# Writing out the batch loops of the attention heads on every engine of a one-core attention and expert kernel

## What is computed

```python
# B, S = 8, 512;  H = 256;  NH = 16;  NOPE, ROPE, VD = 128, 64, 128;  QR, KVR = 128, 64
norm_q  = rmsnorm(x @ W_cq, q_scale)
q_nope, q_rope = norm_q @ W_dq_nope, norm_q @ W_dq_rope        # per head
norm_kv = rmsnorm(x @ W_ckv, kv_scale)
k_nope, value = norm_kv @ W_dk_nope, norm_kv @ W_dv            # per head
k_rope  = x @ W_krope                                          # one for all heads
query = concat([q_nope, rope(q_rope)]);  key = concat([k_nope, rope(k_rope) / NH])
scores = where(causal, query @ key.T / sqrt(NOPE + ROPE), -1e9)
out = softmax(scores) @ value @ W_o                            # 16 heads, 8 batches
x = x + out + ffn(layernorm(x))                                # experts and shared expert
```

## Time and profile before

| what | value |
|---|---|
| median of three runs | 1854.5 us (1851.81 to 1855.62) |
| profiled execution, its own time | 1855.27 us |
| span of the profiled execution | 1853.5 us |
| mean granted clock of PE | 0.895 |
| busy: PE, PEld, DVE, ACT, POOL | 1467.5, 1248.0, 1115.1, 930.9, 569.7 us |

### The profile page before, as it was taken

How to read it: one execution, slowest core, us unless ns; L and a number is a source line. 1 busy time by engine, 2 the same in 40 slices (tenths; PEclk the granted TensorE clock), 3 DMA queues, 4 the chain that set the end, 5 groups by cost and what they waited for, 6 DMA issues and landing times. The chain is left out here.

```text
span 1853.5 us, 37109 instructions
## 1 busy us (share of the span) xinstructions
PE 1467.5 (79%) x10112; PEld 1248.0 (67%) x10113; DVE 1115.1 (60%) x4335; ACT 930.9 (50%) x2739; POOL 569.7 (31%) x640
## 2 busy tenths in 40 slices
PE   2663499989899999999999986799998888885340
PEld 2552378868688777878878764588887777774330
DVE  2896276656566676766666644555555666664464
ACT  1330276656566666666666644366665555552000
POOL 1120043433343343433433430000001433335565
PEclk8676699999999999999999997799999998998665
DMA  3993611321411111111111107654545665665553
GB/s 143 329 375 123 232 56 56 113 88 47 147 58 60 49 52 60 58 62 58 58 54 47 50 21 239 201 163 157 159 153 163 197 184 183 193 194 179 148 168 112
DMA packets 169539, 240.29 MB, mean 130 GB/s; under 512 B 16786, under 2 KB 142738, under 8 KB 165010
## 3 DMA queue, kind: packets, MB, share of 16 engines
q1 hardware_dynamic: 146322, 183.61, 29.9%
q0 software_dynamic: 18432, 50.36, 8.8%
q10 hardware_dynamic: 4608, 4.20, 0.8%
HBM read 115.42 MB, written 122.68 MB: 128 GB/s over the span
## 5 line engine op out<-in xcount | busy, mean ns | idle before, releaser
L988 ACT ACTIVATE prob<-prob,negmax 128x512 f32<-128x512 f32 (+3 forms) x512 | 285.3, 559 | 302.1 <-DVE negmax L1066 300.8
L1066 DVE CUSTOM_DVE_ANT_0 prob<-ps,mask_add 128x512 f32<-128x512 f32 (+3 forms) x512 | 244.2, 485 | 147.4 <-issue 144.2
L61 PE MATMUL ps<-kt_hi,qt_hi 128*128 (+4 forms) x512 | 188.5, 368 | 21.7 <-issue 18.7
L816 POOL DMA_INDIRECT sorted_x<-xn_row,row_no x192 | 188.3, 981 | 49.4 <-issue 45.0
L826 POOL TENSOR_TENSOR spread<-rinv,one 128x512 f32<-128x512 f32 x64 | 66.6, 1040 | 380.0 <-DVE rinv L1072 380.0
L63 PE MATMUL ps<-kt_hi,qt_lo 128*128 (+4 forms) x512 | 166.4, 325 | 0.0
L62 PE MATMUL ps<-kt_lo,qt_hi 128*128 (+4 forms) x512 | 166.0, 324 | 0.0
L910 PE MATMUL ps<-ident,prob 128*128 128x128 f32 x1280 | 160.6, 273 | 0.0
L926 PE MATMUL ps<-pt,nkv 128*64 128x512 f32 (+3 forms) x1024 | 152.0, 439 | 2.3 <-DVE lat L1084 2.3
L910 PEld LDWEIGHTS ps<-ident,prob 128*128 128x128 f32 x1280 | 143.5, 140 | 0.2 <-ACT prob L988 0.2
L1001 ACT ACTIVATE pt<-ps 128x1024 f32<-128x1024 f32 (+2 forms) x130 | 130.4, 1003 | 19.8 <-PE ps L910 16.9
(11 more groups left out here) (240 smaller groups left out, 4481.4 us busy)
## 6 DMA issues: line engine op xcount, KB each, us to landing
sorted_x<-zeros SPq DMA_DIRECT2D x16, 2048.0 KB, 9.4
rows_in<-sorted_x SPq DMA_DIRECT2D x128, 256.0 KB, 2.8
sorted_y<-rows_out SPq DMA_DIRECT2D x128, 256.0 KB
nqt<-nqt_dram SPq DMA_DIRECT2D x16, 512.0 KB
raw_gu<-in_wgu SPq DMA_DIRECT2D x16, 384.0 KB, 4.0
x_in<-in_x SPq DMA_DIRECT2D x8, 512.0 KB, 4.2
xn_dram<-xn SPq DMA_DIRECT2D x8, 512.0 KB, 5.0
xnt_dram<-xnt_hi SPq DMA_DIRECT2D x16, 256.0 KB, 4.7
```

The source lines that it names most:

```text
L61: pe.matmul(out, lh, rh, start=first, stop=False, **kw)
L816: pool.indirect_dma_start(sorted_x, bass.IndirectOffsetOnAxis(ap=row_no[par][:, k:k + 1], axis=0), xn_row[par][:], None).then_inc(scattere ...
L988: act.activation(prob[:, i, qt, 0:w], prob[:, i, qt, 0:w], ACT.Exp, bias=negmax[:, i, qt:qt + 1], scale=-1.0, accum_out=rowsum[:, g // 2 % ...
L1066: dve.tensor_tensor_reduce(prob[:, i, qt, 0:w], s_ps[k % 2][:, 0:w], mask[:, S - w:S], -1.0, -MASKED, ALU.add, ALU.min, negmax[:, i, qt:qt ...
```

## The change

```diff
         def run(eng):
             def batches(first, last):
-                with eng.Fori(first, last) as b:
+                for b in range(first, last):
                     for g in range(NH // 2, NH):
                         step(Batches(b, None, b + 1), g)
                     for g in range(NH // 2):
```

## The result

The changed kernel takes 1821.82 us (median of four runs, 1820.2 to 1824.25), the kernel before 1853.15 us beside it (1850.81 to 1855.62). The ratio is 0.9832, 95% interval [0.9813, 0.9851], a gain of 31.3 us. A second comparison on another chip, where both kernels run faster, gave 1755.58 against 1784.45 us, ratio 0.9843 [0.983, 0.9857], a gain of 28.9 us.

What follows compares the result with a forecast made beforehand. PE was taken to fill the heads stage, stalling at jumps back for instructions. Jumps gave 27.57 us, all other terms 0: 1855.27 - 27.57 = 1827.7 us, given as 1827.5, range 1821 to 1836 us.

Steps and rivals of the forecast that it cites:

- Jumps back: Heads loop: removing six taken jumps on PE, VectorE and ScalarE saves 27.57 us, each priced against the 106.93 us stretch.
- the two rules weighed there: Jump price: about 108 ns per compare-and-branch, 0.65 us for six, or a block fetch at far taken branches, which was favoured.
- the first two were dear: First two heads jumps, 8.76 us each: instructions queue behind SP's two 2 MB zero fills.
- the third jump: Third jump back in the heads: costs PE 1.49 us idle, with VectorE named as releaser; priced 1.80 us.
- Register and branch instructions: Heads loop: REGISTER_ALU and ISA rows, such as 97 and 24 on PE per pass, lie behind queued matmuls; worth 0.
- part 5: Code behind the heads at other addresses: expert loop L1549 has PE branches of 76 to 220 ns, no stall; 0.
- Sequential fetch: Heads: seven bodies read once instead of one read seven times; body already fetched anew each pass, so price 0.
- Rival C: Heads: written-out code cannot be fetched fast enough, about 42 packets at 2.33 us each; slower, 1925.6 us; chance 0.04.
- The row load under the fills: Step 8 row load comes earlier, inside the fills in two batches: up to 4.1 us late, absorbed by GpSimd's idle 4.20 us; 0.
- Rival B: Saving comes, but the row load exceeds GpSimd's slack (1836 us) or a loop behind the heads stalls (1838 us); chance 0.12.
- rival A: Heads turns: the jump costs only the branch, the stall is a wait for late data and stays; 1854.8 us; chance 0.03.
- Place of the code behind: Code behind the heads at other addresses: 0, upper end 3.56 us for each of three taken jumps of L1549 and L1552.

Runs made afterwards that it cites:

- padded: Changed kernel with GpSimd's batch loops kept and 352 one-element memsets per pass added to its body; 1760.21 us, against 1755.14 us for the control with GpSimd written out too.

## Why the prediction was right

**Jumps back, 27.57 us.** Right. The stretch that crosses the same turn without a jump was the right yardstick: its 106.93 us are the 106.95 us of every written-out pass. Measured: 27.42 us in the profiles compared. That the two agree to 0.2 us says no more than this, since both take the 776.1 us from the same profile of the kernel before. What the term did not say is that it is one execution's figure. The second profile of that kernel has 22.4 us over the same yardstick; about 3 us of the difference lie at jumps that held PE in one of the two and not in the other.

**The time itself** came out 5.7 us below the forecast, with a mechanism that is right. 1.9 us of this are the kernel before, which the forecast put at 1855.1 us and whose median beside the change was 1853.15 us; 3.8 us are gain that is not in the sum. The range held it by 0.8 us, thanks to the 3 us allowed for gains that no row shows. That is luck more than foresight.

Of the two rules weighed there, the Trainium skill's Runtime: NRT & Kernel Launch, Instruction fetch mechanics, is borne out for VectorE, ScalarE and, once padded, GpSimd; for PE only in part, since its body was at times still at hand after the jump. The Trainium skill's Advanced Engine Details and Errata, Control Flow Timing, prices the branch alone, and that would have given 0.65 us where 22.4 to 27.4 us were measured.

**Why the first two were dear.** Right: moving the fills brought all jumps to 2.2 to 2.4 us.

**Several engines together.** The prediction took the third jump as VectorE's and the rest as PE's without pricing them apart. The two split kernels showed 21.6 us still lost with VectorE and ScalarE looped and 27.0 us with PE looped. So most of the price was there on either side alone, and a change to PE only would have gained 5.8 us at most in the heads.

**Register and branch instructions, 0.** Right in the heads: 19.43 us twice had said so, and passes without them take 106.95 us, as the one with them had. That the sorted-tile loops cost nothing either, as part 5 and the expectation for all loops had it, was wrong: without them the kernel is 13.8 us faster.

**Sequential fetch, 0.** The price is right, in the heads (no pass of 748.7 / 7 stands out) and in the kernel with every loop written out. Rival C falls. But the argument that PE's body is fetched anew in every pass already holds only for passes behind a jump that held PE; behind another one q8 moved nothing (818 to 926 us in the second profile of the kernel before).

**The row load under the fills, 0.** Right, and close: 7.09 us measured where 7.52 us was the bound, 3.26 us of idle time on GpSimd, 2.44 us left before the spread. Rival B falls, and so does rival A, whose wait at the turn would have stayed.

**Place of the code behind, 0.** No loss seen: the sorted-tile stage took 472.9 us before and 471.3 us after. The 3.6 us that the first pair of profiles has outside the seven passes were not in the forecast; on the second chip the whole gain was 28.9 us. They may be variation of the other stages, and their cause stays open.

## What to carry to other kernels

Compare a pass that ends in a taken jump with one that falls through: the difference is the price of the loop, in the kernel's own time. Take it from more than one execution: here it was 27.4 us in one and 22.4 us in another. When several engines stall at their jumps back, write the loop out on all of them at once, since the stalls run side by side and freeing one side gains little: 5.8 us at most here, of 27.4. Where a loop must stay, keep large DMA transfers away from its jump: here that alone gave 12.7 us, where writing out gave 28.9 us.

## What the runs showed of the hardware

Between two jumps of the heads' loop the trace has 61 instructions on GpSimd, 299 on ScalarE, 396 on VectorE, and on PE 1697 with its weight loads and 768 matmuls (the section on the change says 704 matmuls). GpSimd goes on 0.1 to 0.2 us after its jumps. On ScalarE and VectorE 2.5 to 2.8 us pass between the branch and the first instruction of the body at each jump in quiet, and 6.5 to 6.7 us under the fills, with the DMA engines busy for 0.96. On GpSimd with 413 instructions it is 3.0 us at the sixth jump and 6.8 us at the first.

PE's branch at the jump lasts 3.5 to 3.8 us in quiet and 7.8 to 7.9 us under the fills in the kernel before, or 0.2 us with nine packets fewer on q8, both in the same kernel.

The loop of the sorted tiles L1549, with 1128 instructions on PE, shows no such branch (0.2 us), yet the stage is 13.4 us shorter when all loops are written out, which a look at branch durations alone misses.
